# Norm work of a graph layer: residuals first, residual rows loaded inside the row's last pair, results turned two rows later

## The reference, cut to what matters

```
x = layernorm(x + L0(x, adj, W));  x = layernorm(x + L1(x, adj, ...))      # x: 4096 x 256, adj: 4096 x 4096

def L0(h, adj, W):
    Wh = h @ W.T
    sim = Wh @ Wh.T / (norms * norms.T + EPS)
    alpha = softmax(where((adj > 0) | eye, sim, -inf), axis=1)
    return alpha @ Wh

def L1(x, adj, ...):
    mask = adj > 0
    agg = mask @ x / max(sum(mask, axis=1), 1)
    return relu(concat(x @ W_self + b_self, agg @ W_nb + b_nb) @ W_comb + b_comb)
```

## Time and profile before

| | |
|---|---|
| median of 3 runs (lowest, highest) | 855.03 us (851.92, 855.54) |
| the profiled execution, its own time | 857.24 us |
| its span | 855.4 us |
| TensorE busy | 98% of the span |
| VectorE busy | 69% |
| ScalarE busy | 41% |
| DMA, mean rate | 173 GB/s |
| granted TensorE clock | 0.999 of full |

### The profile page before, as it was taken

The page is one execution under the profiler, slowest core; times in us unless marked ns, Lnnn a source line. Parts: engine busy times, 40 slices in busy tenths (PEclk is TensorE's granted clock), DMA queues, the critical chain, the costliest instruction groups (busy, mean ns, idle before and its releaser), DMA issues.

```text
span 855.4 us, 18019 instructions
## 1 busy us (share of the span) xinstructions
PE 835.1 (98%) x6703; PEld 668.4 (78%) x6703; DVE 587.6 (69%) x1416; ACT 354.9 (41%) x581; POOL 71.6 (8%) x177
## 2 busy tenths in 40 slices
PE   8999999999999999999999999989999999999997
PEld 6767777777777677777776777668888888888886
DVE  2867887889788788889888989898345333333333
ACT  4857665675565555555555646455110000000000
POOL 2400000000000000000001100111101011110111
PEclk9999999999999999999999999999999999999999
DMA  7965675459999999899999998997103321330300
GB/s 189 263 159 151 172 179 164 131 182 236 252 220 237 231 244 259 205 265 232 246 244 195 259 262 216 251 198 237 42 8 130 118 73 64 118 111 20 117 20 20
DMA packets 202862, 147.93 MB, mean 173 GB/s; under 512 B 137505, under 2 KB 169778, under 8 KB 201746
## 3 DMA queue, kind: packets, MB, share of 16 engines
q1 hardware_dynamic: 202578, 146.33, 65.4%
q0 software_dynamic: 192, 0.41, 0.2%
HBM read 95.83 MB, written 20.99 MB: 137 GB/s over the span
## 4 chain that ended last, share of the span: by engine, by line
issue 80%; PE 8%; POOL 6%; DVE 2%; ACT 2%; DMA 1%; POOLq 1%; SPq 0%; DVEq 0%; ACTq 0%
POOL rstd L618 4%; PE ps L1313 2%; POOL var_eps L616 2%; PE ps L1403 1%; PE ps L1405 1%; PE ps L1404 1%; DMA unitT_lo<-feat 1%; PE ps L1343 1%; PE ps L1345 1%; PE ps L1344 1%; PE ps L1397 1%; ACT mask L689 0%; SPq L434 0%; ACT rows L631 0%; ACT feat L643 0%
## 5 line engine op out<-in xcount | busy, mean ns | idle before, releaser
L1403 PE MATMUL ps<-feat,prob_hi 128*128 128x257 f16 x1024 | 280.2, 274 | 3.2 <-DVE prob_lo L1100 2.2
L1405 PE MATMUL ps<-feat,prob_lo 128*128 128x257 f16 x1024 | 279.3, 273 | 0.0
L1404 PE MATMUL ps<-feat,prob_hi 128*128 128x256 f16 x1024 | 278.3, 272 | 0.0
L1573 PE MATMUL ps<-big,mgroup 128*128 128x257 f16 x992 | 219.2, 273 | 0.0
L1574 PE MATMUL ps<-big,mgroup 128*128 128x256 f16 x992 | 219.2, 273 | 0.0
L677 ACT ACTIVATE work<-ps 128x512 f32<-128x512 f32 (+2 forms) x144 | 79.7, 555 | 109.0 <-PE ps L1345 105.5
L1403 PEld LDWEIGHTS ps<-feat,prob_hi 128*128 128x128 f16 x1024 | 99.7, 97 | 29.5 <-DVE prob_lo L1100 3.0
L1404 PEld LDWEIGHTS ps<-feat,prob_hi 128*128 128x128 f16 x1024 | 100.4, 98 | 25.4
L717 ACT ACTIVATE mask<-work 128x1024 fp8e4<-128x1024 f16 x84 | 86.2, 1049 | 68.4 <-DVE work L1094 68.4
L1343 PE MATMUL ps<-unitT_lo,unitT_hi 128*128 128x512 f16 (+3 forms) x288 | 103.7, 362 | 6.4 <-DVE work L971 4.8
L1405 PEld LDWEIGHTS ps<-feat,prob_lo 128*128 128x128 f16 x1024 | 99.5, 97 | 13.5
(11 more groups left out here) (130 smaller groups left out, 959.8 us busy)
## 6 DMA issues: line engine op xcount, KB each, us to landing
adj_sb<-adjT SPq DMA_DIRECT2D x128, 512.0 KB, 4.8
mask_spill<-mask SPq DMA_DIRECT2D x128, 128.0 KB, 4.4
mgroup<-mask_spill SPq DMA_DIRECT2D x8, 2048.0 KB, 8.6
xres<-x SPq DMA_DIRECT2D x8, 512.0 KB, 6.6
out<-rows SPq DMA_DIRECT2D x32, 128.0 KB, 1.7
feat<-xT SPq DMA_DIRECT2D x7, 512.0 KB, 7.5
norm_bc<-norm_row_dram SPq DMA_DIRECT2D x7, 256.0 KB, 4.1
mgroup<-mgroup SPq DMA_TRANSPOSE x84, 3.9
```

The lines of the kernel that those rows point to most:

```text
L1403: pe.matmul(acc(D + 1), prob_hi[:, s, cols], feat_hi_of(g)[:, r, 0:D + 1], start=start, stop=False)
L1404: pe.matmul(acc(D), prob_hi[:, s, cols], feat_lo_of(g)[:, r, :], start=False, stop=False)
L1405: return pe.matmul(acc(D + 1), prob_lo[:, s, cols], feat_hi_of(g)[:, r, 0:D + 1], start=False, stop=stop)
L1573: pe.matmul(agg_ps(q, D + 1), lhsT, z_hi_of(g)[:, r, 0:D + 1], start=(jb == 0), stop=False)
```

## The change

It has four parts.

1. `norm_work`: the list is still 17 pieces, but now runs: `softmax_scale`; the four residuals; `moments` of block 0; then for each q `moments` of block q+1, `normalised` of q, `split_x1` of q-1. The split lags one step behind `normalised` for every row.
2. `load_residual(a)`: for rows 1 to 6 the xres load is issued in the row's last pair, after unit m = 1, ahead of units 2 and 3. For rows 0 and 7 it stays.
3. `turn_x1`: the two transposes of row a-1 are no longer issued at the end of row a. For a = 2 to 5, one half of row a-2 is issued at the end of pair (a, a+1), the other at the end of pair (a, a+2). At the end of row 6, rows 4 and 5 are turned, one after the other.
4. ScalarE in row 6 issues the first `x1_head` of row 5 after the mask of unit 2, not before it.

```
+            def turn_x1(a, halves=range(2)):
+                sync.wait_ge(x1_ready, (a + 1) * GB)
+                for h in halves:
+                    sync.dma_start_transpose(x1T_of(a, h).rearrange("p b k i -> p (b k) i"), x1_half_of(a, h)).then_inc(x1T_loaded[a], 16)
+
+            def load_residual(a):
+                wait(sync, summed_ready, a * GB)
+                sync.dma_start(xres[:, :, :], x_v[a]).then_inc(xres_loaded, 16)
...
+                    if b == G - 1 and m == 1:
+                        load_residual(a)
+                if 2 <= a < G - 2 and b - a <= 2:
+                    turn_x1(a - 2, [b - a - 1])
...
-                wait(sync, summed_ready, a * GB)
-                sync.dma_start(xres[:, :, :], x_v[a]).then_inc(xres_loaded, 16)
-                if 0 < a < G - 1:
-                    turn_x1(a - 1)
+                if a in (0, G - 1):
+                    load_residual(a)
+                if a == G - 2:
+                    turn_x1(G - 4)
+                    turn_x1(G - 3)
...
+                unit_kept(u0 + 2, 2, 4 * k + 3)
                 if early_x1:
                     x1_head(a - 1, 0)
-                unit_kept(u0 + 2, 2, 4 * k + 3)
-                if early_x1:
                     x1_head(a - 1, 1)
...
-                lag = 1 if a < ACT_X1 else 2
-                for q in range(GB + lag):
+                for q in range(GB):
+                    pieces.append(lambda q=q: residual(a, q))
+                pieces.append(lambda: moments(a, 0))
+                for q in range(GB + 2):
+                    if q + 1 < GB:
+                        pieces.append(lambda q=q: moments(a, q + 1))
                     if q < GB:
-                        pieces.append(lambda q=q: residual(a, q))
-                        pieces.append(lambda q=q: moments(a, q))
+                        pieces.append(lambda q=q: normalised(a, q))
                     if 0 < q <= GB:
-                        pieces.append(lambda q=q: normalised(a, q - 1))
-                    if q >= lag:
-                        pieces.append(lambda q=q: split_x1(a, q - lag))
+                        pieces.append(lambda q=q: split_x1(a, q - 1))
```

## The result

The changed kernel takes 849.79 us (median of 10 runs, 849.08 to 851.92) against 855.08 us for the kernel before (10 runs beside it). The ratio is 0.9943, 95% interval 0.9932 to 0.9953: 0.57% faster, 5.3 us. Forecast were 849.5 us and a gain of 5.5 us.

What follows compares the result with a forecast made beforehand. TensorE, busy 98%, was taken as the bound, with 7.6 us idle in rows 1 to 6. Gains of 3.3 + 2.3 us less 0.1 gave 5.5 us, from 855.03 to 849.5 us; range 846.5 to 854.0.

Steps and rivals of the forecast that it cites:

- What bounds it: Whole kernel: TensorE, busy 98% of the span; its 7.6 us idle in rows 1 to 6 cap the first layer's gain.
- The xres load: Diagonals of rows 2, 4 and 5: the earlier load removes TensorE's idle 1.24 + 1.19 + 0.87 = 3.3 us.
- queue bound: Row 1's xres load: 1.3 MB less queued ahead at 236 GB/s is 5.5 us, so it lands about 282.4.
- pessimistic bound: Row 1's xres load: issued 2.7 us sooner with the same 7.3 us to land, so it lands at 285.2.
- The reserve of 1.0 us: At the diagonals: a VectorE wait for xres of under 1.0 us costs TensorE nothing.
- The new order as the condition: SP's wait before the early load: free with four residuals at indices 1 to 4; the old order would hold SP.
- Row 6: VectorE bounds row 6; starting the pair 2.48 us sooner, less 0.2 us for the new order, gains 2.3 us.
- The moved turns: Result turns ahead of far turns in rows 2 to 5: 1.3 us later together, covered by reserve, so cost 0.
- the reserve of 1.9 us: Far part's second transpose at the tightest place: lands at 478.9, first used at 480.82, so 1.9 us to spare.
- rival A: Rows 2 to 5: result turns hold the far turns, seven places lose 1.4 us each, 859.3 us in all; chance 0.07.
- Row 7's burst: Row 7: value tails of groups 0 and 1 come 0.4 to 0.7 us later; 0.1 us taken in the sum.
- Row 0's wait: Row 1's diagonal: VectorE's wait for row 0's xres was expected to stay; no cost was given.

Runs made afterwards that it cites:

- the kernel with the light row 5: The changed kernel with row 5's four bn_stats reading 16 of 256 columns, so row 5 is normalised by their moments: 849.98 us, ratio 0.9932.

## Why the prediction was right, by its own steps

**What bounds it.** Right. 5.6 of the 7.6 idle us went, and by the starts nothing outside rows 1 to 6 gained. That 5.5 us came within 0.2 us of the 5.3 between the medians is partly luck. The sum was read from an execution 2.2 us above its median, and in that same pair of executions rows 1 to 6 gained 6.3 us.

**The xres load.** Right in place and in what it gave: outside row 6 the three idle times of 3.3 us are gone whole. The landing lies between the two bounds. The queue bound said 282.4 for row 1's load and 282.2 was measured, but that is luck, because by then the profiled execution after runs 1.1 us ahead. Measured against the moment at which VectorE comes to the residual, the five loads landed 1.2 to 2.5 us late before and 0.7 to 2.5 us early after. They moved by 4.6, 3.6, 4.8, 2.5 and 4.3 us, where the pessimistic bound has 2.7 and the queue bound 5.5. The queue bound divides its 1.3 MB by the mean rate of the window; while row 1's load was under way in the kernel before (280 to 287 us) the DMA engines moved 322 GB/s, at which 1.3 MB are 4.1 us, by estimate. That the load is the cause, and not the order or the turns, is shown by doing each alone: only the early load makes the kernel faster, and by itself it gives the whole gain.

**The reserve of 1.0 us.** Right for the diagonals of rows 2 to 5. Two more kernels give the same difference between VectorE's wait for xres and TensorE's idle time: 1.94 and 0.80, 3.09 and 1.96, 2.31 and 1.35 with the new order alone; 2.81 and 1.67, 2.80 and 1.84 with the moved turns alone. It lies between 0.96 and 1.14 us each time. By the starts it is a little less, 0.79 to 0.98 us, and the waits of 1.27 us (kernel before, row 3's diagonal, which the prediction put at nothing) and 1.22 us (the later load) cost 0.3 us each. In row 6 the reserve holds only at the diagonal. From VectorE's first residual there to the start of the first turned block on TensorE it is 18.19 or 18.20 us in ten of the twelve profiles, so each us that VectorE loses at the diagonal arrives at that block.

**The new order as the condition.** Here the step was too strong. The prediction said that without the new order the load's wait "would hold SP". It doesn't in this kernel: the early load alone gives the whole gain. In row 6, the tightest place, the fourth residual ends when SP comes to the load, to within 0.03 us.

**Row 6.** The size is right: idle TensorE in row 6 and at row 7's diagonal was 1.51 + 0.33 + 1.57 + 0.47 = 3.88 us and is 1.21 + 0.28 = 1.49, so 2.4 us against 2.3. Its parts are off: the idle time at the first turned block fell only to 1.21, where 0.9 was said, and two smaller ones made up for it. The 0.2 us for the new order were not there: the 18.2 us to the first turned block are the same with the old order (kernel before and the early load alone) and the new. The reason given, VectorE as the bound, holds up to that block by half a us. Both kernels that take work off VectorE ahead of it get there in 17.7 us, and no sooner.

**The moved turns.** Taken at 0. In the medians that is so: the kernel without them is no slower and no faster. SP was held 1.6 us by such a turn in row 4 (464.94 to 466.56), less than the 3 us assumed, and the next far turn went out at 468.84. But the reserve of 1.9 us was read at the wrong place. It is that of a pair's first part; the second part in row 4's last pair had none, already before the change. There the second transpose of L490 goes out at 494.71 in the kernel before and lands at 499.18, and VectorE uses it at (kernel before):

```profile
499.21 0.43 DVE L1099 TENSOR_TENSOR prob_hi<-work,mgroup 128x512 f16<-128x512 f16 x1
```

So every us that this landing comes later is a us of waiting on VectorE. Of the seven profiled kernels with moved turns all but the changed kernel's first profile show such a wait there: 0.30, 0.44, 0.74, 0.87, 1.29 and 1.35 us. The five kernels without them, the one before among them, show 0.15 at most. TensorE has a reserve of its own behind it, as rival A had it: it is idle for 0.27, 0.39, 0.81 and 0.87 us behind the four longest, 0.47 or 0.48 us less each time. So the moved turns cost 0 to 0.9 us of TensorE there, by execution. A result turn goes out 8.3 us ahead of the delayed turns (480.80 and 489.14 in the changed kernel), but in the kernel with both halves together it is 22 us ahead and 0.30 us remain. How the delay is carried that far wasn't settled.

**Row 7's burst.** Taken at 0.1. The value tails of group 1 end 0.47 us before the values of group 3 start, where they had 0.77 us. TensorE shows no idle time, so it cost nothing.

**Left out.** Row 0's wait. It was 0.65 us before, with nothing behind it; 1.46 us in the changed kernel, with 0.39 us of idle TensorE; 0.69 to 1.00 in the others that load it at the row's end, with none. It varies by execution about the reserve. The prediction named this wait among those that stay, but gave it no price.

## What to carry to other kernels

When the bound engine is busy 98% of the time, list its few idle times, name the engine that released each, and ask what that engine itself was waiting for: here 10.3 us of waiting for one 512 KB load at five diagonals, on an engine busy 69% of the time, were behind nearly all the gain there was. What the waits cost was less than their sum, by a reserve of about 1 us each. Move a late load ahead of bulk transfers that nobody needs soon, and bound its landing from both sides: by the same time to land, and by the bytes that it passes. Here four of five loads moved by an amount between the two bounds worked out for row 1, and the fifth by 0.2 us less than the lower. Look for the reserve of what is pushed back at every place where it is used, not at one. Test the parts of such a change singly, since only one of the three did the work here, and one by itself made the kernel 0.4% slower.

## What the runs showed of the hardware

The landing time of one and the same 512 KB load goes with its place among SP's transfers. It is 7.3 us (median of five) with three adjacency loads still under way at its issue, 6.8 with two (the kernel with the load one unit later), and 5.6 with one. The Trainium skill (DMA: Bandwidth & Descriptors, Queues, rings and completion order) has descriptors consumed in ring order on each DMA engine. The landing times agree with that: in none of the twelve profiles does one of SP's 438 transfers land before one that was issued ahead of it.

A result turn of 256 KB takes SP 1.6 to 2.3 us to issue in the seven places of the changed kernel that have a pair behind them, and 2.0 to 3.9 at the ends of rows 1 to 5 in the kernel before; with little under way, as at the end of row 6 there, it takes 1.2 to 1.3. Not expected were the far turns in row 4's last pair: two transposes took SP 5.1 us to issue in the slowest case (the kernel with the light row 5), where the changed kernel and the one before took 3.7, and that 8 us after the last result turn.
